# A spare fill of 128x320 behind each indirect transfer on GpSimd, in a two-layer language-model tower

## The reference

```
h = gated sum of three embedding tables of 25000 x 75, by token id
h = h + linear_attention(layernorm(h))        # 8 heads, tanh/cos/sin features
h = h + merged_ffn(layernorm(h))              # FFN weights mixed per sequence
h = h + gated_causal_attention(layernorm(h))  # 8 heads of 64, cumulative decay
xn = layernorm(h); probs = softmax(xn @ gate) # 8 experts
top 2 experts per token: out += p_e * (gelu(xn @ w1[e] + b1[e]) @ w2[e] + b2[e])
h = h + out
```

## Time and profile before

| what | us |
|---|---|
| three runs | 424.30, 424.38, 423.45; median 424.3 |
| span of the profiled execution | 446.6 |
| TensorE busy in it | 386.1 |
| VectorE busy | 296.5 |
| ScalarE busy | 218.7 |
| GpSimd busy | 134.1 |

### The profile page before, as it was taken

How to read it: one execution, slowest core, us unless ns; L and a number is a source line. 1 busy time by engine, 2 the same in 40 slices (tenths; PEclk the granted TensorE clock), 3 DMA queues, 4 the chain that set the end, 5 groups by cost and what they waited for, 6 DMA issues and landing times.

```text
span 446.6 us, 9131 instructions
## 1 busy us (share of the span) xinstructions
PE 386.1 (86%) x2864; PEld 304.2 (68%) x2864; DVE 296.5 (66%) x947; ACT 218.7 (49%) x460; POOL 134.1 (30%) x139
## 2 busy tenths in 40 slices
PE   2572869998999999999999999999999999349975
PEld 2341758584568965688545895589999998349865
DVE  1477997889999779886899868972277331026205
ACT  1227484934892345422463237954376574126512
POOL 6771044133222411022458102520013005700270
PEclk9997788999999999999999999999999999559999
DMA  5899500000000000000029221010000323111211
GB/s 158 323 376 426 216 1 1 1 1 0 1 1 1 1 1 1 1 1 2 12 88 325 84 60 45 24 48 1 4 0 31 97 79 102 53 35 43 84 53 53
DMA packets 24021, 31.71 MB, mean 71 GB/s; under 512 B 4377, under 2 KB 18720, under 8 KB 22696
## 3 DMA queue, kind: packets, MB, share of 16 engines
q1 hardware_dynamic: 21416, 25.62, 16.5%
q0 software_dynamic: 2560, 5.52, 4.1%
HBM read 18.15 MB, written 12.98 MB: 70 GB/s over the span
## 4 chain that ended last, share of the span: by engine, by line
PE 64%; DVE 12%; ACT 6%; another core or an unknown queue 6%; issue 5%; POOL 3%; DMA 2%; DVEq 0%; ACTq 0%; POOLq 0%
PE bank L1063 8%; PE bank L1052 7%; PE bank L926 5%; PE bank L939 4%; PE bank L955 4%; PE bank L978 3%; PE bank L971 3%; PE bank L963 3%; PE bank L893 2%; PE bank L873 2%; PE bank L911 2%; PE bank L1015 2%; PE bank L887 2%; PE bank L920 2%
## 5 line engine op out<-in xcount | busy, mean ns | idle before, releaser
L1268 ACT ACTIVATE arena<-bank,arena 128x128 f32<-128x128 f32 x168 | 47.5, 369 | 50.5 <-PE bank L1052 27.9
L1063 PE MATMUL bank<-big,arena 128*128 x336 | 47.3, 287 | 16.1 <-DVE h L1620 7.5
L1063 PEld LDWEIGHTS bank<-big,arena 128*128 128x128 f32 x336 | 43.1, 201 | 17.5 <-issue 17.3
L718 POOL DMA_INDIRECT dealt<-xy,arena x28 | 30.0, 1073 | 40.0 <-DVE arena L1655 32.7
L1714 DVE COPY w1s<-big 128x512 f32 x42 | 17.8, 425 | 36.5 <-PE bank L1052 14.6
L926 PE MATMUL bank<-xT_f,wq 128*128 128x512 f32 x64 | 29.0, 595 | 0.5 <-DVE lb L1532 0.5
L734 POOL DMA_INDIRECT vv<-experts_out,arena x16 | 15.1, 943 | 32.9 <-issue 32.9
L1546 DVE TENSOR_TENSOR arena<-bank,causal 128x512 f32<-128x512 f32 x32 | 20.3, 681 | 4.0 <-PE bank L939 4.0
L926 PEld LDWEIGHTS bank<-xT_f,wq 128*128 128x128 f32 x64 | 11.8, 190 | 14.9 <-issue 13.4
L1052 PE MATMUL bank<-arena,w1s 128*128 128x128 f32 x160 | 21.1, 276 | 0.0
L1078 ACT ACT_TABLE_LOAD x16 | 20.5, 1283 | 1.1 <-PEq L1811 0.8
(11 more groups left out here) (283 smaller groups left out, 989.8 us busy)
## 6 DMA issues: line engine op xcount, KB each, us to landing
dealt<-lb SPq DMA_DIRECT2D x7, 1024.0 KB, 13.4
big<-in_tv SPq DMA_DIRECT2D x2, 2048.0 KB
big<-in_ew SPq DMA_DIRECT2D x16, 256.0 KB, 3.1
arena<-dealt SPq DMA_DIRECT2D x20, 64.0 KB, 1.8
experts_out<-arena SPq DMA_DIRECT2D x5, 256.0 KB, 2.6
wq<-in_wq SPq DMA_DIRECT2D x1, 1024.0 KB, 17.7
out<-h SPq DMA_DIRECT2D x4, 256.0 KB
fs<-dealt SPq DMA_DIRECT2D x8, 64.0 KB, 1.9
```

Of the source, the lines that this page charges most:

```text
L718: pool.indirect_dma_start(xs[b // LEAD], bass.IndirectOffsetOnAxis(ap=goal[b][:, k, t:t + 1], axis=0), xy[b % 2][:, t, :], None).then_inc( ...
L1063: last = pe.matmul(p[:, 0:D], hid[n % 2][:, c * P:(c + 1) * P], big[:, bass.ds(e * FF + (E * FF + c * D), D)], start=(c == 0), stop=(c == ...
L1268: last = act.activation(hid[n % 2][:, c * P:(c + 1) * P], of("K.up", n)[:, c * P:(c + 1) * P], ACT.Gelu, bias=eb1[:].rearrange("p e c -> p ...
```

## The change

GpSimd gets a spare tile `blank` of 128x320 float32 and a semaphore for it. Behind every indirect transfer but the four of gather(0) it fills that tile with zeros, then goes on to the next. No one reads the tile. Ahead of each fill it waits for the fill before it.

```diff
+        blank = sb("blank", [P, 320])
+        s_blank = ctx.enter_context(nc.semaphore("s_blank"))
...
+            rests = [0]
+
+            def rest():
+
+                if rests[0]:
+                    pool.wait_ge(s_blank, rests[0])
+                pool.memset(blank[:], 0.0).then_inc(s_blank, 1)
+                rests[0] += 1
...
                         bass.IndirectOffsetOnAxis(ap=idx[:, b * T + t:b * T + t + 1], axis=0)).then_inc(s_gather[b], 16)
+                    if b:
+                        rest()
...
                                 xy[b % 2][:, t, :], None).then_inc(s_deal[b], 16)
+                            rest()
...
                                 bass.IndirectOffsetOnAxis(ap=posi[g][:, k, at:at + 1], axis=0)).then_inc(s_yg[b], 16)
+                            rest()
```

## The result

The changed kernel takes 437.19 us (median of 4, 436.58 to 438.24) against 424.34 for the kernel before; the ratio is 1.0316, with a 95% interval of 1.0294 to 1.0339. The forecast was 431.9, the range 425.0 to 440.0.

The account below looks back on a forecast made before the run. With TensorE's standstills taken out, the prediction held that the gathers bound the end. Start 12r - 0.4 plus end 26r gave 38r - 0.4 = 7.6 us, added to 424.3: 431.9, range 425.0 to 440.0.

Parts of the forecast that it names:

- rival (a): GpSimd's transfers: the gap behind a fill stays 0.30, r = 0.36, cost 13.3 us, time 437.6; chance 0.20.
- rival (c): Third scatter burst: fills block VectorE operations with both sides in SBUF, adding at most 2.9 us, 434.8; chance 0.11.
- The freed timeline: Profile without TensorE's standstills beside Y0, Y1 and in J: span 422.7 instead of 446.6, gathers bounding the end.
- Rival (d): K31 to K41 and J: fills let TensorE's signals through, giving back at most 2.9 us of standstills; chance 0.06.
- The step: GpSimd, transfer to transfer: from 1.25 us to 1.46, as 0.95 transfer, 0.36 fill and 0.15 gap.
- r: GpSimd: how much one fill stretches the time from one indirect transfer to the next; forecast 0.21 us.
- The reading by spacing: Fill counted by start-to-start spacing, about 0.30 us: r = 0.15 and a total of 5.3 us instead of 7.6.
- rival (b): GpSimd's transfers: the fill hides under the gap, r 0 to 0.05, time 423.9 to 425.8; chance 0.13.
- The start: 12 fills ahead of the power delay VectorE's L1365: 12r - 0.4 = 2.1 us, not given back later.
- The end: Gathers of Y: 15 fills ahead of Y1's last transfer, 11 more ahead of Y3's; end moves 26r = 5.5 us.
- Both landings already decide: Y1's landing sets when the last store and Y2 start, Y3's sets the final work, so 26r counts whole.
- The scatters: Fills behind the scatters of sequences 0 to 3 cost nothing; without covers 1.7, 1.7 and 0.6 us.

Follow-up runs that it names:

- second profile of before: The kernel before, unchanged, profiled again: 424.07 us in one run, span 422.3.
- the other form: Kernel before with VectorE's 32 min operations written as scalar_tensor_tensor: 429.23 us; the same with fills behind the 28 scatters: 430.38 us.

## Why the prediction was right in part

The direction and both places that I had counted were right, and 437.2 lies in the range; the size was 7.6 us where 12.9 was measured. That the range holds it is luck: its upper part was there for a dearer step (rival (a)), which did not come, and rival (c), which did, was priced at 434.8 at most.

- **The freed timeline**: right. The standstills were in one recorded execution and not in the others. Rival (d) falls: in the second profile of before TensorE does not stand still there, so there was nothing for a fill to let through. What made the standstills in that execution stays open.
- **The step**: the mechanism was right, the gap behind a fill is 0.16 (forecast 0.15), but the fill has 0.38, not 0.36, and the step is 1.49, not 1.46. With r = 0.245 instead of 0.21 the sum 38r - 0.4 is 8.9, 1.3 more than forecast. The reading by spacing (r = 0.15) was the worse one here. A short fill fits into the gap without a releaser: with 128x1 the whole fill was hidden, r = 0. That is rival (b) for another width; at 320 columns it did not come.
- **The start**, 12r - 0.4 = 2.5 with the measured r: the run with it alone gave 2.6, the trace 2.3, of which 2.0 stand at L1365 (forecast 2.1).
- **The end**, 26r = 6.4: measured 5.5 alone and 5.3 in the trace. "Both landings already decide" was wrong by a hair: there were 1.0 and 0.2 us of cover. With the double width the same sum comes out within the interval.
- **The scatters**, "each costs nothing": this is the step that failed, by 5.3 us in the trace and 6.2 in the run with them alone. I checked who waits for GpSimd, and there the covers held. I did not put VectorE's operations beside the fills into the sum, but only into rival (c), with 2.9 at most in the third burst and nothing for the first two, though the first has three such operations too. Rival (c) is what happened: in the traces 2.0 us in the first burst and 1.9 in the third, 2.2 in the run with the third alone, and next to nothing once the operation has the other form. That is 3.9 of the 5.3. Of the rest, 0.7 is a fall of the clock that profiles without a fill there show as well, 0.2 stands beside it up to the third burst, and 0.55 between the fourth and Y0, of which 0.2 and 0.4 are also found in the two profiles with fills at Y only.
- Rival (a), a gap that stays at 0.30, did not come, although the time is that of its sum: 437.6 forecast by it, 437.2 measured. Only the step in the trace tells the two apart.

## What to carry to other kernels

When work is added on GpSimd, two questions stand apart: who waits for its results, and what runs on VectorE at the same time. Slack on GpSimd's own path covers the first and not the second. Look for VectorE operations of the copy or tensor_scalar kind, with both sides in SBUF, beside every new fill, above all where VectorE runs without a gap (a copy of 128x8 took 0.46 instead of 0.17 in the first burst); a row where such an operation of four elements takes 1.09 us tells what a fill can do to it. And before the sum is made against a span that is 5% above the runs' median, find out where the difference lies, or take a second profile. Before a step between two single traces is called an effect, look for it in the trace of a kernel that is unchanged there.

## What the runs showed of the hardware

- A min of 128x512 in the tensor_scalar form took 0.96 or 0.97 us instead of 0.43 where, by the rows, it began in an indirect transfer and reached into the fill of 128x320 behind it: six times in the trace after, each time by the same 0.54, which is more than the fill's own 0.38. Two others in that trace ran beside a transfer only, and took 0.75 (288.74, the first of the third burst, where the kernel before has 0.43) and 0.43 (242.21). A fill of 128x1 left it at a mean of 0.45. The two engines fell into step: scan and min together took 2.13, and so did transfer, fill and gap (228.29 to 230.41 on GpSimd, whose transfer is then 1.43 and its fill 0.53). Why it is 0.54 and not the length of the fill, or what part of it the transfer ahead holds, is not settled.
- A fill of one column (0.11) fits into the 0.30 between two indirect transfers with no loss, and behind a fill of 320 columns 0.16 of it is left.
- TensorE's granted clock can fall to half for 3.2 us and more in one execution and not in the next, at the same place of the same program: at L926 it was 1.00 in the second profile of before and 0.50 with fills at Y only, with no wait of TensorE ahead of either. A difference under 1 us between two single traces can be this.
- One recorded execution of the kernel before lost some 24 us to standstills of TensorE beside bursts of indirect transfers; none of the profiles taken since did (spans of 421.9 to 436.9, each 1 to 2 us below its run's time).
